# Linear attention on one core: the last but one chunk's output projection stands in the tail, around the last mean squares; the last squares go by blocks and the last residual has a tile of its own

## The reference, cut to what matters

```python
q, k, v = (silu(xn @ W) for W in (Wq, Wk, Wv))         # xn = layernorm(x)
o = lightning_attn(q, k, v, log_decay)                 # chunks of 128 tokens, a state per head
gate = (xn @ Wg1) @ Wg2
o = o * sigmoid(gate)                                  # "og"
o = o * rsqrt(mean(o * o over each head) + 1e-5) * norm_w
x = x + o @ Wo + glu_ffn(xn)                           # Wo: the output projection
```

## Time and profile before

| what | us |
|---|---|
| median of 3 runs | 1769.5 (1769.17 to 1769.53) |
| the profiled execution's own time | 1764.4 |
| its span, first to last instruction | 1762.7 |
| PE / DVE / ACT / POOL busy | 1567.7 / 988.6 / 603.4 / 648.5 |
| mean granted TensorE clock | 0.945 of full |

### The profile page before, as it was taken

How to read it: one execution, slowest core, us unless ns; L and a number is a source line. 1 busy time by engine, 2 the same in 40 slices (tenths; PEclk the granted TensorE clock), 3 DMA queues, 4 the chain that set the end, 5 groups by cost and what they waited for, 6 DMA issues and landing times. The chain is left out here.

```text
span 1762.7 us, 22247 instructions
## 1 busy us (share of the span) xinstructions
PE 1567.7 (89%) x7890; PEld 1088.6 (62%) x7890; DVE 988.6 (56%) x1698; ACT 603.4 (34%) x1138; POOL 648.5 (37%) x530
## 2 busy tenths in 40 slices
PE   5998888899999999997979999489999964799997
PEld 4886544454545545444767777367777753688886
DVE  7664766777888778833535545355565361132332
ACT  3211245555555555562212212354232320122221
POOL 4000034276887688682256666252021010000000
PEclk9998789999999999998989999789999986899999
DMA  6876513644536445134621121342022015420210
GB/s 228 269 231 186 116 23 82 124 101 90 152 103 139 111 132 119 49 102 166 228 91 60 54 73 49 111 149 73 30 91 96 1 49 185 155 96 1 95 48 24
DMA packets 99029, 188.51 MB, mean 107 GB/s; under 512 B 28890, under 2 KB 37994, under 8 KB 97050
## 3 DMA queue, kind: packets, MB, share of 16 engines
q1 hardware_dynamic: 77044, 120.60, 24.4%
q0 software_dynamic: 13648, 51.61, 9.9%
q10 hardware_dynamic: 8234, 14.94, 2.4%
HBM read 121.97 MB, written 65.16 MB: 106 GB/s over the span
## 5 line engine op out<-in xcount | busy, mean ns | idle before, releaser
L999 ACT ACTIVATE att_probs<-att_ring 128x512 f32<-128x512 f32 (+3 forms) x640 | 298.4, 537 | 287.6 <-DVE att_ring L1036 148.4
L1027 DVE TENSOR_REDUCE att_maxes<-att_ring 128x2 f32<-128x1024 f32 (+7 forms) x366 | 339.0, 947 | 83.8 <-PE att_ring L921 75.0
L956 PE MATMUL att_outp<-att_probs,att_vs 128*64 128x512 f32 (+3 forms) x1280 | 277.4, 556 | 0.3 <-ACT att_att L982 0.3
L1592 PE MATMUL glu_u<-glu_xh,glu_w 128*128 128x512 f32 x352 | 139.5, 396 | 19.9 <-DMA glu_xl<-zn_lo 19.9
L956 PEld LDWEIGHTS att_outp<-att_probs,att_vs 128*64 128x64 f32 x1280 | 79.7, 139 | 122.8 <-issue 72.7
L1593 PE MATMUL glu_u<-glu_xl,glu_w 128*128 128x512 f32 x352 | 139.2, 395 | 0.0
L1651 DVE TENSOR_TENSOR glu_hid<-glu_sig,glu_u 128x512 f32<-128x512 f32 x44 | 30.3, 688 | 170.4 <-ACT glu_sig L1631 170.4
L1665 POOL DMA_DIRECT2D out<-glu_y x4 | 3.1, 787 | 314.5 <-DVE glu_y L1656 253.8
L921 PE MATMUL att_ring<-route_wbh,route_wah 100*128 100x512 f32 (+2 forms) x320 | 104.7, 411 | 14.3 <-PEq L57 6.4
L942 PE MATMUL att_ring<-route_wah,route_wbh 102*128 102x512 f32 (+2 forms) x320 | 106.5, 410 | 10.2 <-ACT att_probs L999 5.5
L921 PE MATMUL att_ring<-moew_wbl,moew_wal 100*128 100x512 f32 (+2 forms) x320 | 99.7, 385 | 15.8 <-ACT att_probs L999 12.1
(11 more groups left out here) (274 smaller groups left out, 3374.2 us busy)
## 6 DMA issues: line engine op xcount, KB each, us to landing
att_q_raw<-in_w POOLq DMA_DIRECT2D x48, 352.0 KB, 4.0
w_ternary<-att_q_out POOLq DMA_DIRECT2D x24, 352.0 KB, 2.6
glu_w<-w_ternary ACTq DMA_DIRECT2D x9, 768.0 KB, 11.9
xn<-qkv_x SPq DMA_DIRECT2D x4, 1024.0 KB, 7.2
q_hi<-qkv_hi SPq DMA_DIRECT2D x16, 256.0 KB, 4.1
q_lo<-qkv_lo SPq DMA_DIRECT2D x16, 256.0 KB, 4.5
k_hi<-qkv_hi SPq DMA_DIRECT2D x16, 256.0 KB, 2.9
k_lo<-qkv_lo SPq DMA_DIRECT2D x16, 256.0 KB, 3.5
```

What stands on the lines that cost most here:

```text
L956: last = pe.matmul(outp[v_cols(h), off:CH], vs[p % 2][:, kt, v_cols(h)], probs[:, g % 4, h, off:CH], start=kt == 0, stop=kt == TT * (c + 1 ...
L999: act.activation(probs[:, g % 4, h, off:CH], ring[:, rg.banks["score", g][h], off:CH], ACT.Exp).then_inc(exped, 1)
L1027: last = dve.tensor_reduce(maxes[:, hs, t, g:g + 1], banks[:, :, 0:width], AX.X, ALU.max)
L1592: pe.matmul(u[:, n % 2, :], w[:, k, s], xh[par][:, k, :], start=k == 0, stop=False)
```

## The change

Chunk 2's output projection leaves its place in chunk 3, between gk and the gate. Its tiles 0 and 1 are computed right behind the last scan, ahead of chunk 3's mean squares, and its tiles 2 and 3 between the mean squares and the spreading of the inverses. The ring's list follows. DVE adds tiles 0 and 1 ahead of chunk 3's inversion and tiles 2 and 3 behind it. ACT squares chunk 3 in four blocks of 128 tokens, each behind the copy of the next tile, the last one behind the scan; PE's mean squares wait for the fourth. SP loads chunk 3's residual into `x` (free once chunk 3's rows are transposed) with a semaphore of its own, `last_in`; chunk 3's output is summed and stored from there, and `y` is stored for the third time in the tail.

```diff
--- before.py
+++ after.py
@@ -1684,6 +1684,10 @@
         for c in range(-1, NCH + 1):
             for kind, count, late in (("q", KT, 0), ("k", KT, 0), ("v", TT, 0), ("gk", 1, 0),
                                       ("norm", TT, -1), ("out", TT, 1), ("turn", KT, 0)):
+                if kind == "out" and c == NCH - 1:
+                    continue
+                if kind == "out" and c == NCH:
+                    order += [(kind, NCH - 2, n) for n in range(count)]
                 if 0 <= c - late < NCH:
                     order += [(kind, c - late, n) for n in range(count)]
         self.order = order
@@ -1755,7 +1759,7 @@
         scored, score_taken = st.sem("scored"), st.sem("score_taken")
         o_taken, decay_ready = st.sem("o_taken"), st.sem("decay_ready")
         gate_made, gate_taken, spread_made = st.sem("gate_made"), st.sem("gate_taken"), st.sem("spread_made")
-        x_in, r_in, z_stored = st.sem("x_in"), st.sem("r_in"), st.sem("z_stored")
+        x_in, r_in, z_stored, last_in = st.sem("x_in"), st.sem("r_in"), st.sem("z_stored"), st.sem("last_in")
         first_in = [st.sem(f"first_in{t}") for t in range(TT)]
         made, taken = st.sem("made"), {e: st.sem(f"taken_{e}") for e in ("act", "dve")}
         qd_ready = st.sem("qd_ready")
@@ -1799,6 +1803,9 @@
                 if c == 0:
                     for j in range(2 * KT, len(ws.pieces)):
                         ws.load(sp, j)
+                if c == NCH - 1:
+                    sp.dma_start(x[:], rows_of(x_d, c)).then_inc(last_in, 16)
+                    continue
                 if c:
                     wait_taken(sp, "out", c - 1, TT - 1)
                     sp.dma_start(rows_of(out_d, c - 1), y[:]).then_inc(stored, 16)
@@ -1806,8 +1813,9 @@
                 else:
                     ws.wait(sp)
                 sp.dma_start(y[:], rows_of(x_d, c)).then_inc(r_in, 16)
-            wait_taken(sp, "out", NCH - 1, TT - 1)
-            sp.dma_start(rows_of(out_d, NCH - 1), y[:]).then_inc(stored, 16)
+            for c in (NCH - 2, NCH - 1):
+                wait_taken(sp, "out", c, TT - 1)
+                sp.dma_start(rows_of(out_d, c), (x if c == NCH - 1 else y)[:]).then_inc(stored, 16)
             sp.wait_ge(stored, NCH * 16)
             sp.wait_ge(z_stored, NCH * 32)
 
@@ -1839,7 +1847,7 @@
                     last.then_inc(made, 1)
 
             def mean_squares(c):
-                pe.wait_ge(squared, c + 1)
+                pe.wait_ge(squared, c + 1 if c + 1 < NCH else c + TT)
                 pe.wait_ge(fresh_ready, (c + 1) * TT)
                 for g in range(KT):
                     last = pe.matmul(mean_sq[g * HD:(g + 1) * HD, :], msel, sq[:, g, :], start=True, stop=True,
@@ -1854,11 +1862,11 @@
                     last = pe.matmul(wide[:, g, :], spread[rows, g * P:(g + 1) * P], inv[rows, :], start=True, stop=True)
                 last.then_inc(spread_made, 1)
 
-            def output(c):
+            def output(c, ts=range(TT)):
                 if c == 0:
                     ws.wait(pe)
                 pe.wait_ge(lo_ready, (c + 1) * KT)
-                for t in range(TT):
+                for t in ts:
                     out, s = slot("out", c, t), slice(t * P, (t + 1) * P)
                     for k in range(KT):
                         last = three_passes(pe, out, ogh[:, k, s], ogl[:, k, s], wh["o"][:, k, :], wl["o"][:, k, :],
@@ -1956,7 +1964,7 @@
                 last.then_inc(made, 1)
                 if c + 1 < NCH:
                     norm_turn(c + 1)
-                if c:
+                if c and c + 1 < NCH:
                     output(c - 1)
                 gates(c)
                 for g in range(KT):
@@ -1971,7 +1979,9 @@
                     attend_before(c, t)
                     for g in range(KT):
                         attend_within(c, t, g)
+            output(NCH - 2, range(0, TT // 2))
             mean_squares(NCH - 1)
+            output(NCH - 2, range(TT // 2, TT))
             spread_inverses(NCH - 1)
             output(NCH - 1)
 
@@ -1983,6 +1993,12 @@
             def square(c):
                 act.wait_ge(gated, (c + 1) * TT)
                 act.activation(sq[:], og[:], ACT.Square).then_inc(squared, 1)
+
+            def square_block(t):
+
+                s = slice(t * P, (t + 1) * P)
+                act.wait_ge(gated, (NCH - 1) * TT + t + 1)
+                act.activation(sq[:, :, s], og[:, :, s], ACT.Square).then_inc(squared, 1)
 
             def take_root(c):
                 act.wait_ge(ms_made, c + 1)
@@ -2058,7 +2074,9 @@
                     if n >= 2:
                         act.wait_ge(gated, n - 1)
                     act.activation(o_copy[:, n % 2].rearrange("p g c -> p (g c)"), o[:], ACT.Copy).then_inc(o_taken, 1)
-            square(NCH - 1)
+                    if c + 1 == NCH and t:
+                        square_block(t - 1)
+            square_block(TT - 1)
             take_root(NCH - 1)
             high(NCH - 1)
 
@@ -2095,10 +2113,14 @@
                     dve.tensor_tensor(xl[:, :, s], arrived(dve, "norm", c, t).rearrange("p (k n) -> p k n", n=P),
                                       xh[:, :, s].bitcast(F32), ALU.subtract).then_inc(taken["dve"], 1)
 
-            def add_output(c):
-                dve.wait_ge(r_in, c * 16 + 16)
-                for t in range(TT):
-                    dve.tensor_tensor(y[:, t, :], y[:, t, :], arrived(dve, "out", c, t), ALU.add
+            def add_output(c, ts=range(TT)):
+                if c == NCH - 1:
+                    dve.wait_ge(last_in, 16)
+                else:
+                    dve.wait_ge(r_in, c * 16 + 16)
+                to = x if c == NCH - 1 else y
+                for t in ts:
+                    dve.tensor_tensor(to[:, t, :], to[:, t, :], arrived(dve, "out", c, t), ALU.add
                                       ).then_inc(taken["dve"], 1)
 
             def decay(c, t, g):
@@ -2154,9 +2176,9 @@
                 if c + 1 < NCH:
                     norm.normalize(dve, c + 1)
                     norm_low(c + 1)
-                if c:
+                if c and c + 1 < NCH:
                     add_output(c - 1)
-                else:
+                elif c == 0:
                     ws.wait(dve)
                 for g in range(KT):
                     if c and g == 0:
@@ -2168,7 +2190,9 @@
                     for g in range(KT):
                         decay(c, t, g)
                     advance(c, t)
+            add_output(NCH - 2, range(0, TT // 2))
             invert(NCH - 1)
+            add_output(NCH - 2, range(TT // 2, TT))
             normalize(NCH - 1)
             add_output(NCH - 1)
 
```

## The result

The changed kernel ran four times at first, with a median of 1755.99 us (1754.78 to 1758.02); four runs of the kernel before, by then, had 1769.51 us (1769.17 to 1770.46). The two profiled executions, however, are 1764.4 and 1754.78 us: 9.6 us apart.

The account below looks back on a forecast made before the run. PE was taken as the bound, with the gate and scan waiting for its projection. Terms of -10.05 and -0.1 gave -10.15 us: 1754.2 against the profiled 1764.4, or 1759.3 from the median; range 1756.3 to 1762.3 us.

Parts of the forecast that it names:

- gate behind gk's copy: Chunk 3: without the projection ahead of it, the gate starts at 1406.55 in place of 1416.62, -10.05 us.
- mean squares start: Tail: the half projection ahead of them delays their start from 1441.78 to 1443.4, +1.65 us.
- their duration: Tail: mean squares take 1.06 us at full clock, not 1.93 at half clock, -0.87 us.
- spreading, its duration: Tail, behind the second half projection: spreading the inverses takes 1.14 us at full clock, not 2.09.
- normalizing starts, net of the gate: Tail: behind DVE's adds of tiles 2 and 3, normalizing starts at 1452.65 instead of 1452.77, -0.1 us.
- squares by blocks: ACT's square ready 1.3 us earlier, but hidden by the half projection: worth 0; 1.3 us without that cover.
- residual's own tile: Separate tile for chunk 3's residual: worth about nothing; without it, load lands at 1463.4 against the first add at 1463.56.
- ramp of the last projection: Half clock until 5.7 us after the last projection starts, costing 2.5 us; same fall and return assumed, so 0.
- sum in the stretch: From ACT's copy of chunk 3's gk to DVE's last add: -10.05 - 0.1 = -10.15 us.
- The covers named for the two edits at zero: Half projection hides the square until 1443.4; residual's store and load would end at 1463.4, before the add at 1463.56.
- The slower rivals: Clock falls before scan (1762.2 us, 0.06) or in tail (1764.1, 0.03); no gain (1769.4, 0.04); slower (1776.8, 0.03).
- The first rival: Last projection finds the clock high, worth up to 2.5 to 2.9 us: 1756.4 to 1756.8 us; chance 0.08.

Follow-up runs that it names:

- whole_square: Changed kernel with one square of 2048 columns behind the last gate product instead of four blocks; median 1757.74 us, gk's copy to last add 54.63 us.
- resid_in_y: Changed kernel without the residual's own tile: chunk 3's residual loaded into y behind the store of chunk 2's sum; median 1758.51 us.
- one_two_one: Changed kernel with chunk 2's projection cut 1 + 2 + 1 around mean squares and spreading; median 1751.54 us (ratio 0.9937 to the kernel before), repeated 1753.10 (0.9913).
- one_two_one_whole_square: The 1 + 2 + 1 cut with one square of 2048 columns in place of four blocks; median 1757.95 us, ratio 0.9933 to the kernel before.

## Why the prediction was right and wrong

| step | forecast, us | measured, us |
|---|---|---|
| gate behind gk's copy | -10.05 | -10.07 |
| mean squares start | +1.65 | +1.60 (5.59 for 3.99 behind the scan) |
| their duration | -0.87 | -0.87 |
| spreading, its duration | -0.95 | -0.95 |
| normalizing starts, net of the gate | -0.1 | -0.28 (DVE's two adds take 1.28, not 1.38, and it starts 0.05 before they end) |
| squares by blocks | 0 | 0 (whole_square); 1.3 without cover |
| residual's own tile | 0, cover just enough | 0 to 0.2 (resid_in_y), 0.7 to spare |
| ramp of the last projection | 0 | +0.16 in one profile, -0.9 to -1.3 in four others |
| sum in the stretch | -10.15 | -10.19 in the first profile; -11.2 to -11.7 in the four with the shorter ramp |

**Right:** the place of every step, their sizes up to normalizing within 0.2 us, the direction, and why: PE was what the scan waited for, and the tail had room for its work. In the tail the three expected signs are there: no gap behind the scan, mean squares at full clock, DVE's adds ending at the spreading's end. The covers named for the two edits at zero are the ones that hold them. The slower rivals did not occur: the clock did not fall ahead of the scan (no fall between 1190 and 1443 in this profile).

**Wrong, first:** "The same difference from the median, 5.1 us higher, gives 1759.3 us", with a range whose own uncertainty was "about +-0.6". Three runs within 0.4 us were read as a kernel that repeats to 0.4 us. The profiled execution of the same kernel, 5.1 us away, stood beside them and said otherwise. The kernel's executions have a standard deviation of 3.9 us, and in the two profiles at hand the stretch had no part in it (65.95 and 65.97 us). The first median of the changed kernel, 1755.99, lies 2.3 us below the mean of its 20 runs, and that of before, 1769.51, 1.35 us above the mean of its 75. These two make 3.65 us: the whole distance between 13.5 and the 9.9 of all runs. The step that failed is the transfer from one execution to a median of few, not a term of the sum. The prediction took the 5.1 us between profiled execution and median over to the changed kernel; there its first four runs showed 1.2 us (1754.78 to 1755.99). The 3.9 us too much, less the 0.5 by which the profiled execution lies above its forecast of 1754.2, are the 3.3 us between 1759.3 and 1755.99. That this profiled execution came so close to 1754.2 is luck too: one execution is as uncertain as the 3.9 us say.

Why the first runs of before lay so close together stays open. Three runs drawn at random from the 53 on chip 0 lie within 0.36 us of each other in about 0.3% of draws; the first ones may not have been independent of each other, or were made under other conditions (the record does not name their chip).

**Wrong, second and smaller:** "I take the same fall and return: 0." The last projection did begin at half clock as before, but in four of five profiles of the changed kernel and the two variants with the same order of PE, the full clock returned sooner, and the stretch was 1.0 to 1.5 us shorter than in the first: something that the sum had as nothing. The first profile's agreement to 0.04 us is that of the one profile of five with the long ramp, in which +0.16 there and -0.18 at normalizing cancel. The first rival (clock high throughout) was the wrong mechanism for it, since the clock fell in all five; full clock throughout took a gap of 2.3 us instead of 5.2, or a filled one.

What is **open**: why the first block's attention takes longer in one execution than in another, whether the kernel before has the shorter ramp in some of its executions, and why the clock fell in one of three profiles with the same 2.3 us gap.

## What to carry to other kernels

Where the scarce engine is full at one place and idle in a chain of small steps a little later, moving independent work of its own into those waits can take nearly the work's whole length off (here 10.2 to 11.7 of the stretch, for a projection of 10.95 us), and it kept the clock high for the steps between. Cut it to the waits, so that what stands ahead of a step ends when the step's input is ready: 1 + 2 + 1 tiles gave 4.1 to 5.5 us more than 2 + 2, and a second speed-up (squares by blocks) only counts in the cut that leaves the engine free. And ahead of any forecast to a few microseconds, compare the profiled execution with the runs: where they differ by more than the runs among themselves, the runs are too few, and that difference belongs in the range.

The best version compared with the changed kernel on one chip in the same rounds is one_two_one: four executions with a mean of 1754.0 us, against 1759.7 in the changed kernel's ten.

## What was not expected of the hardware

The granted clock's low stretches have lengths that repeat: 23.9 us in both profiles of before (1439.8 to 1463.7, and 1443.6 to 1467.5), 10.2 us in the first profile after, and 6.8 us in the four others with that order of PE. In the tail of nine profiles the clock fell 1.1 to 4.1 us after PE's last matmul, in a gap; in one_two_one_whole_square it fell 0.6 us after work had resumed, so a gap can cost half clock even when it is over before the fall.

The last projection started at the same distance behind gk's copy, within 0.02 us, in the two executions of the changed kernel set side by side above, and yet ran at half clock for 6.1 us in one (14 matmuls started in them) and 3.35 us (8 matmuls) in the other. So the price of a ramp differs between executions of one program, here by 1.3 us. The Trainium skill ("TensorE: Matmul & The Clock Gate", section "What's actually happening") says that the number of slow matmuls at the start of a burst changes from run to run, because the chip's own measuring does not begin with the work. These two executions agree with the first part; no run here isolates the reason.
